# A two-hop graph product on one core: the columns of panel pairs turned into seven block products, and the order of five groups changed with it

## The reference, cut to what matters

```python
h = relu(layernorm(x))                                  # 5120 x 64, fp32
u = par_u[0] * par_u[1] * (diag_u[:, None] * h[:2048] @ W_u) + h[:2048]
i = par_i[0] * par_i[1] * (diag_i[:, None] * h[2048:] @ W_i) + h[2048:]
e = concatenate([u, i])
g = adj @ (adj.T @ e)                                   # adj: 5120 x 5120, dense fp32
out = x + layernorm(g) * ln_gamma + ln_beta + h
```

## Time and profile before

| | |
|---|---|
| median of 3 runs | 371.7 us (371.28 to 372.43) |
| profiled execution, its own time | 371.32 us |
| its span, first to last instruction | 369.5 us |
| granted TensorE clock, mean | 0.997 |
| PE busy | 360.3 us, 98% |
| DVE / ACT / POOL busy | 263.0 / 74.3 / 159.6 us |
| data moved | 133.22 MB, mean 361 GB/s |

### The profile page before, as it was taken

How to read it: one execution, slowest core, us unless ns; L and a number is a source line. 1 busy time by engine, 2 the same in 40 slices (tenths; PEclk the granted TensorE clock), 3 DMA queues, 4 the chain that set the end, 5 groups by cost and what they waited for, 6 DMA issues and landing times.

```text
span 369.5 us, 10865 instructions
## 1 busy us (share of the span) xinstructions
PE 360.3 (98%) x4776; PEld 151.7 (41%) x4776; DVE 263.0 (71%) x282; ACT 74.3 (20%) x213; POOL 159.6 (43%) x94
## 2 busy tenths in 40 slices
PE   7998999999999999999999999999999999999994
PEld 4664454543323443443334334334433343344432
DVE  5999994999061969395677839694956768385266
ACT  5863022010050004001300500040023005002422
POOL 2023060020019902970793199049607931990036
PEclk9999999999999999999999999999999999999998
DMA  8999999999999978989898989889898989853933
GB/s 311 422 419 415 418 426 419 419 419 402 403 380 411 363 291 331 427 343 411 323 429 331 419 326 425 338 318 421 349 409 326 427 339 413 325 247 132 426 130 142
DMA packets 19897, 133.22 MB, mean 361 GB/s; under 512 B 2209, under 2 KB 2977, under 8 KB 4001
## 3 DMA queue, kind: packets, MB, share of 16 engines
q1 hardware_dynamic: 19440, 132.22, 88.1%
q10 hardware_dynamic: 432, 0.66, 0.5%
HBM read 131.55 MB, written 1.31 MB: 360 GB/s over the span
## 4 chain that ended last, share of the span: by engine, by line
PE 87%; DMA 7%; POOL 2%; SPq 2%; DVE 1%; issue 0%; ACT 0%; DVEq 0%; POOLq 0%
PE h_acc L887 36%; PE t_acc L918 24%; DMA natural<-adj_rows 7%; PE x_acc L955 7%; PE h_acc L975 7%; PE t_acc L856 5%; PE t_acc L955 5%; PE h_acc L870 2%; POOL xs L424 1%; SPq L289 1%; POOL sums L420 1%; PE t_acc L993 1%; DVE xs L795 0%; SPq L286 0%; DVE sums L784 0%
## 5 line engine op out<-in xcount | busy, mean ns | idle before, releaser
L599 DVE STREAM_TRANSPOSE strips<-natural 128x2048 f32<-128x2048 f32 x76 | 169.0, 2279 | 48.2 <-PE h_acc L887 48.0
L887 PE MATMUL h_acc<-strips,tokens 32*64 32x512 f32 x2432 | 133.5, 589 | 0.1
L918 PE MATMUL t_acc<-natural,e 128*32 128x512 f32 x832 | 92.3, 592 | 0.1
L887 PEld LDWEIGHTS h_acc<-strips,tokens 32*64 32x64 f32 x2432 | 53.3, 132 | 79.4 <-issue 74.3
L399 POOL TENSOR_TENSOR sums<-natural 128x1024 f32<-128x1024 f32 x14 | 33.3, 2381 | 113.4 <-DMA natural<-adj_rows 113.4
L918 PEld LDWEIGHTS t_acc<-natural,e 128*32 128x32 f32 x832 | 27.4, 110 | 59.4 <-issue 58.2
L955 PE MATMUL x_acc<-sums,forms 128*32 128x256 f32 x280 | 41.1, 380 | 0.0
L856 PE MATMUL t_acc<-natural,e 128*64 128x256 f32 x320 | 36.5, 382 | 1.4 <-DMA natural<-adj_rows 1.1
L489 ACT COPY smalls<-x_acc 32x256 f32<-32x256 f32 x7 | 2.6, 365 | 170.1 <-PE t_acc L955 170.1
L479 ACT COPY tokens<-tokens 32x384 f32<-32x384 f32 (+2 forms) x60 | 24.2, 403 | 51.6 <-DVE tokens L623 30.9
L407 POOL TENSOR_TENSOR sums<-natural,sums 128x1024 f32<-128x1024 f32 x14 | 33.3, 2379 | 1.1
(11 more groups left out here) (97 smaller groups left out, 299.8 us busy)
## 6 DMA issues: line engine op xcount, KB each, us to landing
natural<-adj_rows SPq DMA_DIRECT2D x100, 1024.0 KB, 7.9
cols<-adj_cols SPq DMA_DIRECT2D x20, 1024.0 KB, 11.6
natural<-adj_last SPq DMA_DIRECT2D x4, 1024.0 KB, 10.8
out<-xs SPq DMA_DIRECT2D x4, 256.0 KB, 2.0
xs<-x ACTq DMA_DIRECT2D x2, 256.0 KB, 5.3
xs<-x SPq DMA_DIRECT2D x2, 256.0 KB, 7.7
out<-xs SPq DMA_DIRECT2D x2, 128.0 KB, 2.0
smalls<-small SPq DMA_DIRECT2D x1, 150.0 KB, 3.6
```

Of the source, the lines that this page charges most:

```text
L599: nc.vector.transpose(strips[:, a, :, m].rearrange("p c t i -> p t c i"), natural[:, a, m].rearrange("p t (c j) -> p t c j", j=Q)).then_in ...
L887: last = nc.tensor.matmul(h_acc[D * s:D * (s + 1), q], t[part, a, b, u, :], rows, start=(isinstance(g, int) and g == 0 and b == 0 and u == 0),
L918: last = nc.tensor.matmul(t_acc[lane, pair_bank(half)].rearrange("p (a w) -> p a w", a=2), e[:, GT * m + 2 * k + s, Q * v:Q * (v + 1)], na ...
```

## The change

Four things are changed together.

1. **The loaded columns of a pair.** `loaded_pair` makes 7 products of 2 x 2 blocks as well: 28 matmuls of 256 columns instead of 16 of 512. The blocks are the two panels of the pair and the two halves of group 4's rows. POOL makes the sums of blocks of `cols` (`add_cols`, four operations of 128 x 1024 for each pair) and the sums of columns of `t` (`form_t`, four of 128 x 64). Four of the seven products of a lane go straight to bank 4 of `h_acc`; the other three are summed over all seven pairs in bank 1 of `t_acc`, which is cleared for it (`clear_products`), and are combined once, in the tail (ACT copies the bank, `combine_products` is 12 DVE operations). `last_columns` of group 1, which uses the same bank, waits for that (`s_cols_whole`).
2. **The residual.** The new sums need 12 KB in each partition. They take the room of `xs`. So `xs` (1.31 MB) is written to the output tensor in memory behind the first refills for pair 3 (`s_spilled`), and read back in the tail (`s_reloaded`) into a free part of `natural`.
3. **The order.** PE takes groups 0 and 4 early, and 3, 1, 2 behind the strips. So the sums of group 4 of a pair are needed at the end of a turn, and those of group 3 at the start of the next. SP's list follows: group 4 of both panels, then 2 (of the panel before), 0, 3, 0, 3, 1, 1, 2, then `cols`; in the first pass for pair 3 it is 4, 4, 0, 0, 3, 3, the write of `xs`, both `cols`, 1, 1, 2.
4. **The turns.** DVE turns seven of eight groups of a pair ahead of the work on `t`, where it was six.

The core of the diff (names and lines are those of the kernel before and after; the clearing, the copies and the semaphores are left out where the text above says them):

```diff
-ORDER = (0, 1, 4, 2, 3)
-EARLY = 2
-TURNS = (0, 1, 3, 2)
-BEHIND = 2
+ORDER = (0, 4, 3, 1, 2)
+TURNS = (0, 3, 1, 2)
+BEHIND = 1
...
             for g in range(PAIRED + 2, PANELS, 2):
                 for a in range(2):
-                    for m in range(EARLY):
-                        refill(g + a, m)
-                for m in (4, 3, 2):
+                    refill(g + a, 4)
+                if g > PAIRED + 2:
+                    refill(g - 1, 2)
+                    refill(g, 0)
+                    refill(g, 3)
+                    refill(g + 1, 0)
+                    refill(g + 1, 3)
+                else:
+                    for m in (0, 3):
+                        for a in range(2):
+                            refill(g + a, m)
+                    sp.wait_ge(s_res, GROUPS)
+                    sp.dma_start(out[:], xs[:]).then_inc(s_spilled, 16)
                     for a in range(2):
-                        refill(g + a, m)
+                        refill_cols(g - 2 + a)
                 for a in range(2):
-                    refill_cols(g - 2 + a)
+                    refill(g + a, 1)
+                refill(g, 2)
+                if g > PAIRED + 2:
+                    for a in range(2):
+                        refill_cols(g - 2 + a)
+            refill(LAST, 2)
...
+            sp.wait_ge(s_spilled, 16)
+            sp.dma_start(res[:], out[:]).then_inc(s_reloaded, 16)
...
+            def add_pair(half):
+                add_blocks(half)
+                form_t(half - 1)
+                pool.wait_ge(s_spilled, 16)
+                add_cols(half - 1)
...
             def first_rest(half):
-                first_summed(half, 4)
-                first_plain(half, 2)
-                first_summed(half, 3)
+                first_summed(half, 3)
+                for m in (1, 2):
+                    first_plain(half, m)
             def first_early(half):
-                for m in range(EARLY):
-                    first_plain(half, m)
+                first_plain(half, 0)
+                if not isinstance(half, int):
+                    pe.wait_ge(s_t_left, LEFT * (half - FIRST_HALF - 1))
+                first_summed(half, 4)
...
             def loaded_pair(half):
                 for a in range(2):
-                    loaded_quarters(2 * half + a, a, half)
+                    pe.wait_ge(s_cols[a], 16 * (half + 1))
+                    pe.wait_ge(s_t, 2 * half + 1 + a)
+                pe.wait_ge(s_cleared, 2)
+                pe.wait_ge(s_t_forms, 4 * (half - FIRST_HALF + 1))
+                pe.wait_ge(s_col_sums, 4 * (half - FIRST_HALF + 1))
+                for i in range(7):
+                    for lane in range(QUADRANTS):
+                        in_place, *others = BY_LANE[lane]
+                        n, h, b = in_place[i] if i < 4 else others[i - 4]
+                        weights_in, columns_in = col_product(n, h, b)
+                        place = h_acc[lane_of(lane), LOADED, columns_of(h)] if i < 4 else \
+                            t_acc[lane_of(lane), 1, columns_of(int(n == 7))]
+                        last = nc.tensor.matmul(place, weights_in, columns_in, start=False, stop=False,
+                                                skip_group_check=True)
...
+                if m == 1:
+                    pe.wait_ge(s_cols_whole, 2)
...
             second_loaded(PAIRED - 1, 1, PAIRED // 2 - 1)
+            pe.wait_ge(s_forms, 4 * len(SUMMED))
             first_early(FIRST_HALF + 1)
-            pe.wait_ge(s_forms, 4 * len(SUMMED))
```

More of the change, by code:

```diff
@@ L212, in form_of, with col_block, col_sum, lane_of @@
             return forms[:, n, HALF * SUMMED.index(m):HALF * (SUMMED.index(m) + 1)]
+        def col_block(s, a):
+            return cols[:, a, s].rearrange("p b c -> p (b c)")
+        def col_sum(n):
+            return col_block(1, 0) if n == 2 else col_sums[:, (0, 1, None, 2)[n]]
+        def lane_of(v):
+            return slice(Q * v, Q * (v + 1))
         def pair_bank(half):
@@ L325, in _ @@
             for g in range(2, PAIRED + 2):
-                for m in range(GROUPS):
+                for m in range(GROUPS) if g < PAIRED else ORDER:
                     refill(g, m)
@@ L522, in _ @@
             spread_pair(FIRST_HALF)
+            act.wait_ge(s_loaded_done, PAIRED)
+            nc.scalar.copy(kept, h_acc[P - Q:P, LOADED]).then_inc(s_kept, 1)
             pairs(act, pair)
+            act.wait_ge(s_loaded_done, 2 * LAST_HALF)
+            nc.scalar.copy(products, t_acc[:, 1]).then_inc(s_products, 1)
             def square_out(m):
@@ L671, in keep_t_pair, with clear_products, combine_products, place @@
                 turn_t(2 * half + 1, 1, slice(WIDE, 2 * WIDE))
+            def clear_products():
+                dve.wait_ge(s_t_sum, PAIRED + 2)
+                nc.vector.memset(t_acc[:, 1], 0.0).then_inc(s_cleared, 1)
+                dve.wait_ge(s_kept, 1)
+                nc.vector.memset(h_acc[P - Q:P, LOADED], 0.0).then_inc(s_cleared, 1)
+            def combine_products():
+                def place(lane, part):
+                    return t_acc[lane_of(lane), 1, columns_of(part)]
+                fifths = h_acc[P - Q:P, LOADED]
+                two, three, four, five = (halfway[lane_of(v)] for v in range(4))
+                lanes = [combined[lane_of(v)] for v in range(4)]
+                dve.wait_ge(s_products, 1)
+                for h in range(2):
+                    nc.vector.tensor_tensor(two[:, columns_of(h)], place(2 + h, 0),
+                                            products[lane_of(h), 0:WIDE], ALU.add).then_inc(s_halfway, 1)
+                for h in range(2):
+                    dve.wait_ge(s_halfway, h + 1)
+                    nc.vector.tensor_tensor(three[:, columns_of(h)], place(2 * h, 1),
+                                            two[:, columns_of(h)], ALU.add).then_inc(s_halfway, 1)
+                for h in range(2):
+                    dve.wait_ge(s_halfway, h + 3)
+                    nc.vector.tensor_tensor(lanes[2][:, columns_of(h)], place(2 * h + 1, 1),
+                                            three[:, columns_of(h)], ALU.add).then_inc(s_halfway, 1)
+                nc.vector.tensor_tensor(lanes[1], fifths, two, ALU.add).then_inc(s_combined, 1)
+                for h in range(2):
+                    nc.vector.tensor_copy(lanes[0][:, columns_of(h)], place(h, 0)).then_inc(s_combined, 1)
+                dve.wait_ge(s_halfway, 6)
+                nc.vector.tensor_tensor(five, fifths, lanes[2], ALU.add).then_inc(s_halfway, 1)
+                dve.wait_ge(s_combined, 3)
+                nc.vector.tensor_tensor(h_acc[0:P - Q, LOADED], h_acc[0:P - Q, LOADED], combined[0:P - Q],
+                                        ALU.add).then_inc(s_cols_whole, 1)
+                dve.wait_ge(s_halfway, 7)
+                nc.vector.tensor_tensor(h_acc[P - Q:P, LOADED], five, kept, ALU.add).then_inc(s_cols_whole, 1)
             def step(g, a, half):
@@ L753, in _ @@
                 centre_e(m)
-            turn_pair(FIRST_HALF, keep_t_plain)
+            for a in range(2):
+                for m in TURNS:
+                    turn_strips(PAIRED + a, a, FIRST_HALF, m)
+            keep_t_plain(FIRST_HALF)
+            clear_products()
             with dve.Fori(FIRST_HALF + 1, LAST_HALF) as half:
```

100 lines of the change are left out of this document (75 added, 25 removed), and 3 rows, old and new, of the table BY_LANE.

## The result

The kernel became slower, by 1.3%, and by more than forecast. The median of six runs is 376.19 us (375.79 to 377.4) against 371.54 of six runs before (371.28 to 372.43): ratio 1.0126, 95% interval 1.0108 to 1.0144. Forecast were 373.2 us, so +4.65 came where +1.5 was expected.

What follows compares the result with a forecast made beforehand. PE was taken as the bound, busy 360.3 of 369.5 us. Terms -2.87 + 1.45 + 1.6 + 1.4 = +1.6 us gave 373.2 us in terms of the median 371.7; own range 372.0 to 375.0, wider range 370.3 to 377.0.

Steps and rivals of the forecast that it cites:

- Seven products: Column block of each of seven pairs: 3.02 instead of 3.43 us, 0.41 less each, -2.87 us on PE.
- POOL, 0 in the settled loop: POOL's sums in the settled loop: some 30 of 33.4 us a turn, hidden by PE's work, cost 0.
- Before the loop: Ahead of the loop: PE waits 0.3 for group 0 and for POOL's sums of group 4, together +1.45 us.
- The first turn: Loop's first turn: queued loads and write delay group 0 of panel 9; 0.8 at full pace, 1.9 by late row, +1.6 taken.
- Later turns: Later loop turns: group 0 of a pair's second panel has 2.2 us of cover against 1.1 of lateness, cost 0.
- The tail: Behind the last block: twelve DVE operations of 5.4 us put PE's first output turn at E + 15.0, +1.4 us.
- The read under its cover: Tail: read of xs, due at POOL's first sum, costs nothing under its cover; without it, at most 1 us.
- the queue that keeps up: Rival, no change: write goes beside the reads or wait at 140 is at most 0.8; 371.7 to 372.5 us, chance 0.27.
- the faster case: Rival: write hidden and either the sums early enough or DVE's tail work fitting; -1.5, 370.2 us, chance 0.13.
- the fetched code: Rival: loop body of 260 matmuls no longer stays, each of five jumps waits 2.0 us; 383 us, chance 0.05.
- the wait that returns each turn: Rival: load of group 0 of the second panel over 2.2 us late in each turn; +6, 379 us, chance 0.08.
- the block that is no faster: Rival: seven waits and operands from four tiles keep the column block at 3.43 us; 376 us, chance 0.07.

Runs made afterwards that it cites:

- experiment 4: Kernel after with the column blocks of the seven pairs computed as before (16 matmuls of 512 columns), all else kept: 379.31 us, ratio 1.0199.
- experiment 1: Kernel after without the write of xs to DRAM and without its read back: 374.02 us, ratio 1.0052.
- Experiment 2: Kernel after with tail edits: products copied and four DVE operations run earlier, 375.84 us; read of xs issued earlier, 376.16 us; both together, 372.94 us.

## Why the prediction was wrong

The waits came where it had them; two terms of its sum, the first turn and the tail, were too small. In its own order:

- **Seven products, -2.87.** Right. Block 3.02 us, turn 33.42 us, and experiment 4 gives the 0.42 a turn back.
- **POOL, 0 in the settled loop.** Right. Its 234.2 us of work, half as much again as before, make no wait in a later turn.
- **Before the loop, +1.45.** Right: strips at 113.56 against 112.37, 1.2 later, although a summed group stands there in a plain one's place (0.4 less). The term is therefore 1.6, from waits of 0.53 and 1.12 us, where 0.3 and 1.2 were forecast.
- **The first turn, +1.6: mis-sized, it was 3.5.** The turn took 150.46 - 113.56 = 36.90 us, 3.48 more than a settled one. The prediction put group 0 of panel 9 at 141.0 on an even pace and it landed at 143.6. From the landing at 105.4 us to this one are 38.2 us, 2.8 more than the even pace of 14.25 transfers. Without the write the 13 transfers took 33.9, 1.7 more than the even pace of 13 (experiment 1), so the write adds 1.1 to 1.3 beyond the 3.1 us of its bytes. The prediction held the write at its bytes and, by choosing 1.6 between an even pace (0.8) and the late row (1.9), allowed 0.8 for all lateness. It also added nothing for the 0.2 us that each wait cost beyond its idle time, twice. The range of the write's price, up to 6.2 us, held the true one; the value chosen did not.
- **Later turns, 0.** Right, no wait for `natural` behind 144 us.
- **The tail, +1.4: mis-sized, it was 2.5.** It begins at the time forecast, 7.5 us behind the last block. DVE's twelve operations take 6.5 instead of 5.4 us. The distance of 0.35 is that of an addition and a transpose behind it. In the twelve, operations of 256 columns start 0.45 apart and those of 512 columns 0.72, and not only where one waits for the one ahead: the second of L782 and the first of L794 wait for none of them, and still start 0.45 and 0.72 us behind the one ahead. Why the transpose starts sooner isn't shown. Eight and four of them are 6.5. The Trainium skill (VectorE: DVE Perf Modes, section The TRN2 errata) has (N + 151) / 0.96 ns for an addition in fp32, 0.42 and 0.69 us here; the trace agrees, with 0.43 and 0.70 for one, and its sum, an estimate of 6.2, would have been nearer than the row taken.
- **The read under its cover.** Right by 0.01 us only. Experiment 2 shows that it took the whole gain of a shorter tail: POOL stood 2.94 us for it.

The tail's right distance stood in the trace of the kernel before, in two additions of 256 columns just behind the row taken, 0.47 us apart:

```profile
140.71 0.43 DVE L666 TENSOR_TENSOR x_acc<-x_acc,smalls 32x256 f32<-32x256 f32 x1
141.18 0.42 DVE L668 TENSOR_TENSOR t_sum<-x_acc,t_sum 32x256 f32<-32x256 f32 x1
```

The terms as measured: -2.87 + 1.6 + 3.5 + 2.5 = +4.7, the difference of the spans. Of the rivals, the queue that keeps up is wrong by experiment 1, and with it the faster case; the fetched code is wrong by turns of 33.42 us without a gap and without a packet of instructions from 144.1 to 321 us, and the wait that returns each turn did not come. The rival of the block that is no faster named 376 us, about what was measured, by luck: its block would have taken 3.43 us and took 3.02. The chances outside the wider range add up to 0.195 and not 0.18.

## What to carry to other kernels

A transfer added to a queue without gaps costs at least its bytes, and here two fifths more, and all of it lands on the first consumer that has no cover, until slack in later turns has paid it back; look for that consumer, and for gaps elsewhere in the queue, before the gain is counted. A chain of short DVE operations is to be priced by the distance of two such operations in a row of the trace, not of one and a transpose. Where two things end within a fraction of a microsecond, shortening one shows nothing: run both edits alone and together. Where a time comes out as forecast, look in the trace whether it came by the forecast's path: with the write issued sooner it did not.

## What the runs showed of the hardware

- A write of 1.31 million bytes from SBUF to DRAM amid loads cost 4.4 us of a queue of 420 GB/s. The pace fell to 276 and 281 GB/s for 3 us right ahead of it in both profiles of the kernel after, and not without the write (418). The packets that were slow are those of the loads (0.4 to 0.6 us on average for 8 KB instead of 0.31); the write's own (10 KB in 0.385 us) were not.
- TensorE's clock fell to 1.2 GHz behind a wait of 1.8 to 2.4 us in some profiles (0.50 from 357 to 363 us; a mean of 0.65 from 107 to 110) and stayed at 2.4 GHz behind like waits in others (2.10 us at 136).
- Behind a wait for a transfer, 32 matmul records of PE took 3.64 us instead of 3.43, after idle times of 0.53, 0.89 and 2.10 us alike.
